# A reordering of a mixture-of-experts stage's blocks, with the next stage's first preparing moved beside its last nine, and four instead of six load seats

## What is computed

```python
x = x + 0.5 * ffn(layernorm(x))     # mixture of experts
x = x + attention(layernorm(x))     # 16 heads of 8, q = k = v
x = x + 0.5 * ffn(layernorm(x))     # the same mixture again

def ffn(x):                         # 4096 tokens, 8 experts, each token goes to its best 2
    xf = layernorm(x, ln_g, ln_b)
    scores, idx = top_k(xf @ router_w, 2)
    gate = softmax(scores)
    # expert e on its tokens: z = layernorm(xf, eg, eb)
    # x2 = clip(z @ W2 + b2); hidden = clip((z @ W1 + b1) * silu(x2)); y = clip(hidden @ Wo + bo)
    return sum over the two experts of gate * y
def attention(x):
    q = (x @ W_qkv.T) split in 16 heads
    return softmax(q q^T / sqrt(8)) q, heads joined, @ W_o.T
```

## Time and profile before

| | us |
|---|---|
| median of 3 runs | 1426.98 |
| the profiled execution's own time | 1427.73 |
| its span, first to last instruction | 1426.0 |
| first block's rows transposed | 108.3 |
| last transposing back of the first mixture | 330.47 |
| first row maximum of the attention on VectorE | 371.76 |

### The profile page before, as it was taken

How to read it: one execution, slowest core, us unless ns; L and a number is a source line. 1 busy time by engine, 2 the same in 40 slices (tenths; PEclk the granted TensorE clock), 3 DMA queues, 4 the chain that set the end, 5 groups by cost and what they waited for, 6 DMA issues and landing times.

```text
span 1426.0 us, 29423 instructions
## 1 busy us (share of the span) xinstructions
PE 1248.9 (88%) x10053; PEld 649.7 (46%) x10053; DVE 1170.2 (82%) x2305; ACT 896.2 (63%) x1876; POOL 511.2 (36%) x595
## 2 busy tenths in 40 slices
PE   3738999984389999999999999999999988889992
PEld 3727888872022222322323323233322247778882
DVE  8876788876698899889898988988899458868885
ACT  1214555552058888888778887788877865545651
POOL 3875333334433000243335324351434023433331
PEclk9999999996589999999999999999999999999997
DMA  8126545451311201102111011011101312445555
GB/s 260 38 71 217 203 180 191 178 204 34 104 51 35 72 19 35 36 24 66 36 40 48 17 57 36 17 52 36 36 3 32 113 62 101 161 170 186 188 204 192
DMA packets 65382, 135.58 MB, mean 95 GB/s; under 512 B 13330, under 2 KB 34932, under 8 KB 65204
## 3 DMA queue, kind: packets, MB, share of 16 engines
q1 hardware_dynamic: 56196, 116.18, 23.7%
q0 software_dynamic: 8704, 16.93, 3.7%
q10 hardware_dynamic: 336, 0.59, 0.1%
HBM read 47.35 MB, written 25.07 MB: 51 GB/s over the span
## 4 chain that ended last, share of the span: by engine, by line
PE 44%; DVE 21%; DMA 3%; issue 3%; ACT 3%; SPq 1%; POOL 0%; ACTq 0%; POOLq 0%; DVEq 0%
PE psum L2067 13%; DVE att_neg_part L1753 11%; PE psum L2043 7%; PE psum L2047 5%; PE psum L2024 5%; PE psum L1971 3%; PE psum L1959 3%; PE psum L1961 3%; DVE att_neg_part L1758 2%; DVE stats L1426 1%; ACT att_probs L1326 1%; DMA y_dram<-ffn_y,ffn_block_rows 1%; PE psum L2090 1%; ACT att_o_t L1341 1%; DMA ffn_rec<-record 1%
## 5 line engine op out<-in xcount | busy, mean ns | idle before, releaser
L1326 ACT ACTIVATE att_probs<-psum 128x512 f32<-128x512 f32 x1024 | 556.5, 596 | 119.3 <-PE psum L2049 90.3
L1753 DVE TENSOR_REDUCE att_neg_part<-psum 128x2 f32<-128x1024 f32 x441 | 532.0, 1223 | 69.0 <-PE psum L2025 56.0
L2067 PE MATMUL psum<-att_probs,att_values 128*16 128x256 f32 x4096 | 321.4, 386 | 6.3 <-ACT att_o_t L1341 4.2
L1281 ACT ACTIVATE ffn_silu<-ffn_x2c,ffn_rec 128x256 f32<-128x256 f32 (+1 forms) x320 | 154.6, 487 | 163.3 <-DVE ffn_x2c L1689 162.6
L1143 POOL DMA_INDIRECT y_dram<-ffn_y,ffn_block_rows x144 | 142.1, 987 | 274.5 <-ACT ffn_y L1299 248.7
L2024 PE MATMUL psum<-att_right,att_left 64*128 64x512 bf16 x512 | 198.3, 388 | 27.5 <-DMA att_right<-q_parts_dram 15.9
L2043 PE MATMUL psum<-att_right,att_left 64*128 64x512 bf16 x512 | 198.6, 388 | 4.9 <-DVE att_neg_part L1753 4.8
L2046 PE MATMUL psum<-att_right,att_left 64*128 64x512 bf16 x512 | 198.5, 388 | 4.0 <-DVE att_neg_part L1753 2.1
L1689 DVE TENSOR_SCALAR ffn_x2c<-psum,ffn_rec 128x256 f32<-128x256 f32 (+1 forms) x320 | 162.8, 513 | 45.9 <-PE psum L1961 41.7
L2025 PE MATMUL psum<-att_right,att_left 64*128 64x512 bf16 x512 | 198.9, 389 | 0.0
L2047 PE MATMUL psum<-att_right,att_left 64*128 64x512 bf16 x512 | 193.7, 378 | 0.0
(11 more groups left out here) (198 smaller groups left out, 1514.4 us busy)
## 6 DMA issues: line engine op xcount, KB each, us to landing
ffn_rec<-record SPq DMA_DIRECT2D x80, 776.5 KB, 3.7
ffn_block_rows<-rows_dram SPq DMA_DIRECT2D x64, 130.0 KB, 2.2
att_left<-q_parts_dram SPq DMA_DIRECT2D x64, 96.0 KB
att_right<-q_parts_dram SPq DMA_DIRECT2D x120, 48.0 KB
record<-in_L_ffn_W SPq DMA_DIRECT2D x16, 256.0 KB, 6.5
last_y<-y_dram SPq DMA_DIRECT2D x8, 512.0 KB, 7.4
att_right<-q_parts_dram SPq DMA_DIRECT2D x90, 32.0 KB
y_dram<-ffn_y,ffn_block_rows POOLq DMA_INDIRECT x144, 2.6
```

The source lines that it names most:

```text
L1326: S.activation(probs[:, slot % PROBS, :], ring_bank(("score", slot))[:, :], ACT.Exp, scale=SCALE).then_inc(att_bank.by_act, 1)
L1753: last = V.tensor_reduce(out=neg_part[:, h % 2, keys, p::PAIR, t], in_=psum[:, low:high + 1, :], axis=AX.X, op=ALU.max, negate=True)
L2067: last = TE.matmul(value_bank[head * VS:head * VS + VW, q], values[:, b % 2, kt, team * TEAM + head, :], probs[:, (UNIT * n + j) % PROBS, ...
```

## The change

1. **Order of blocks.** The 8 singles now stand at i = 23 to 30 (`SINGLES`), and 9 pairs follow. Among an expert's pairs, those that hold rows of the first batch come first, so that everything of the first batch is done when block 30 is. The layout on VectorE works with 16 instead of 8 running sums for this. Both mixtures use this order.
2. **Seats.** The first mixture has 4 seats instead of 6 (`SLOTS = (4, 6)`), its buffers lie elsewhere in SBUF so that the attention's first operands fit beside them; the second keeps 6.
3. **Loads.** `sync_next_block` now loads the weights as soon as the seat's old block is `biased`, and then waits for its scatter to load the rows. Before, both waited for the scatter, and the rows came first.
4. **Chores.** The first batch's preparing (`PREPARED`) becomes a list `HEAD`: GpSimd's first blankings stand beside blocks 23 to 26, steps 0 to 15 beside blocks 34 to 38. SyncE loads the first batch's results behind the load of block 34, and the first team's operands behind the load of block 39. The two attention weights are loaded and transposed at the program's start.

```diff
-    SECTIONS = [slice(0, EARLY), slice(EARLY, PAIRS), slice(PAIRS, BLOCKS)]
-    SLOTS = 6
+    LEFT = E - 2
+    SINGLES = slice(EARLY + LEFT, EARLY + LEFT + E)
+    SECTIONS = [slice(0, EARLY), slice(EARLY, SINGLES.start), SINGLES, slice(SINGLES.stop, BLOCKS)]
+
+    KINDS = [(BH, 0, 0), (BH, 1, 0), (1, 2, 0), (BH, 1, LEFT)]
+    SLOTS = (4, 6)
...
-        def seat(i):
+        def seat(k, i):
-            return (i - 1) % SLOTS
+            return (i - 1) % SLOTS[k]
...
+        HEAD = [[] for _ in range(HC * (BLOCKS - SINGLES.start))]
+        for n in range(4):
+            HEAD[4 * n].append(("blank", n, 0, WHOLE))
+        at = HC * E
+        for step, half, slot in ((0, 0, 15), (1, 0, 15), (0, 1, 16), (1, 1, 16), (2, 0, 17), (2, 1, 18), (11, 0, 23), (11, 1, 25)):
+            HEAD[at + slot].append(("prepare", 0, step, (half, 2)))
+        for step, slot in ((3, 19), (5, 20), (7, 21), (9, 22), (13, 27), (15, 28)):
+            HEAD[at + slot].append(("prepare", 0, step, WHOLE))
...
             for i in range(EARLY, BLOCKS):
                 sync_next_block(k, i)
+                if k == 0 and i == SINGLES.stop + SLOTS[0] - 1:
+                    sync_first_results()
+            if k == 0:
+                sync_first_team()
...
         def sync_next_block(k, i):
-            n = k * BLOCKS + i - SLOTS
-
+            n = k * BLOCKS + i - SLOTS[k]
+
+            Q.wait_ge(biased, n + 1)
+            sync_load_record(k, i)
             Q.wait_ge(scattered_y[n % YSETS], y_scatters(n + 1, n % YSETS))
             sync_load_rows(k, i)
-            sync_load_record(k, i)
...
-            pool_blank_values(0)
-            pool_blank_left(0)
-            for chore in PREPARED:
-                pool_chore(*chore)
-            pool_blank_right(0)
-            G.wait_ge(split_done, 1)
-            pool_blank_values(1)
             for s in range(1, OPERANDS):
                 pool_blank_left(s)
                 pool_blank_right(s)
```

More of the change, by code:

```diff
@@ L244, in build_macaron @@
         first = ExitStack()
-        sets.extend(RouteSet(k, first) for k in range(1, B - 1))
-        beyond = sbuf("beyond_the_blocks", [P, 4096], owner=first)
-        sets.append(RouteSet(B - 1, first))
+        last_set = RouteSet(B - 1, first)
         VEC = 2 * E + 2 * E * HC + E
@@ L337, in build_macaron @@
         laid_out = semaphore("laid_out")
-        block_in = [semaphore(f"block_in{s}") for s in range(SLOTS)]
         scattered_y = [semaphore(f"y_scattered{r}") for r in range(YSETS)]
@@ L782, in sync_experts @@
                 sync_load_rows(0, 0)
-                for i in range(1, SLOTS):
+                for i in range(1, SLOTS[0]):
                     if i >= 2:
@@ L789, in sync_experts @@
                 sync_fillers(0)
-            for i in range(SLOTS, EARLY):
+            for i in range(SLOTS[k], EARLY):
                 sync_next_block(k, i)
@@ L1006, in pool_program @@
             for n in range(2):
-                for some, tiles in zip(SECTIONS, (BH, BH, 1)):
-                    G.iota(blocks_i[:, n, some], pattern=[[tiles if n else 1, some.stop - some.start]], base=0,
-                           channel_multiplier=0)
+                for some, (tiles, _, past) in zip(SECTIONS, KINDS):
+                    G.iota(blocks_i[:, n, some], pattern=[[tiles if n else 1, some.stop - some.start]],
+                           base=past * (tiles if n else 1), channel_multiplier=0)
             G.iota(spares_i[:, :], pattern=[[1, BH]], base=RESULTS, channel_multiplier=BH)
@@ L1073, in pool_chore @@
                 G.tensor_tensor(rows, rows, projected(half), ALU.add).then_inc(x_by_pool, 1)
+            elif what == "blank" and which < 2:
+                pool_blank_values(which)
+            elif what == "blank" and which == 2:
+                for lane in sets[B - 1].rows_out:
+                    G.wait_ge(lane, 16 * BT)
+                pool_blank_left(0)
+            elif what == "blank":
+                pool_blank_right(0)
             elif what == "mix":
@@ L1356, in scalar_chore @@
                 h = (step // 2 - 1) % 2
-                S.wait_ge(*att_bank.full(("prepare", which, step)))
+                S.wait_ge(*when_full(("prepare", which, step)))
                 if which > 1:
@@ L1970, in tensor_second @@
             for c in range(HC):
-                last = TE.matmul(y_bank[n % 2][:, few], rec[:, s, WO + c * F:WO + (c + 1) * F], hidden[:, n % 2, c, few],
+                last = TE.matmul(y_bank[n % 2][:, few], mix[k].rec[:, s, WO + c * F:WO + (c + 1) * F], mix[k].hidden[:, n % 2, c, few],
                                  start=(c == 0), stop=(c == HC - 1))
```

302 lines of the change are left out of this document (167 added, 135 removed).

## The result

The changed kernel takes 1521.59 us, median of 4 runs (1518.04 to 1527.56), against 1426.82 for the kernel before, also 4 runs. The ratio is 1.0666, 95% interval 1.0628 to 1.0704. The profiled execution took 1527.56 us, its span is 1525.8 (1426.0 before).

What follows compares the result with a forecast made beforehand. TensorE bounds the first mixture at 5.62 us a pair; four seats would bind instead at 9.0. Terms 3.8 + 108.5 + 7.5 + 8 - 36.7 + 7.8 + 2 = +100.9 gave 1528 us, range 1490 to 1565.

Steps and rivals of the forecast that it cites:

- The seat's cycle: First mixture: weighing, scatter, row load, transposing and copy close over one block with four seats; 9.0 us per pair against 5.62.
- Singles: First mixture's single blocks: steps of 7.1 us among themselves, 8.6 or 7.5 where singles and pairs meet.
- Chores: Preparing moved beside the first mixture's last blocks: the first rstd holds block 32's scatter some 5.6 us; +8, ends 3 and 16.
- Middle: First mixture, block 4's to block 39's transposing: +116.5 us, from +108.5 for the steps and +8 for chores.
- The hole: Between the first mixture's last landing and the first row maximum: closed whole, operands loaded ahead; -36.7 us.
- Drain: Block 39's transposing to the last landing: 21.8 us with a pair, against 14.3 with a single; +7.5.
- The attention's start: First row maximum to first score: 34.9 instead of 27.1 us, SyncE's loads standing behind GpSimd's blanking; +7.8.
- GpSimd's blankings: Beside the first mixture's blocks: two of 1.8 us each time fit between scatters, whose two issues take 2.3 of 9.0 us.
- Second mixture: Six seats kept: drain grows by 7.5 us, earlier weights are credited 5.5; +2, ends -5 and +8.
- The pace holds: Rival, first mixture: landing and loading stay hidden, steps stay at 5.62 us or the singles' pace; 1418 us, chance 7%.
- The clock falls as well: Rival, first mixture: waits drop TensorE to half clock, steps of 11.2 us; +53, 1581 us, chance 5% for the large loss.
- A lighter load makes landings shorter: Rule against the trace, scatter landings: slower pace shortens them to 2.1 us, giving 1511 instead of 1528 us.

Runs made afterwards that it cites:

- the seats mended: Changed kernel with separate row seats in the first mixture, weights kept at four: five row seats 1.0026, six with weights issued early 1.0013 of the kernel before.

## Why the prediction was right, point by point

- **The seat's cycle, 9.0 us per pair.** Right in mechanism, 5% long. Measured 8.53: weighing to request 5.66 (taken 5.96), request to transposing 2.13 (2.2), to the copy 0.47 (0.48), to the weighing 0.27 (0.37). That the circle closes over one block is shown by the runs: 8.7 us with four seats in either order, 5.62 with five or six. The 0.3 in the first part lie behind the second scatter's issue: from there to the rows' request it is 2.97 instead of 3.27. The landing goes with it: over 140 to 300 us the view of the line has 2.2/2.3/3.4 (least, median, most), in the kernel before over the same stretch 2.2/2.7/5.6.
- **Start, +3.8.** +2.0: from the first transposing to block 4's it is 3.6 us more, but the first transposing itself came 1.65 earlier.
- **Singles.** Steps of 8.05 behind pairs and 6.5 to 6.8 among themselves, forecast 8.6 and 7.1: the same 0.5. The step to block 26 is the exception (9.66).
- **Chores, +8 (3 to 16).** Mis-sized, inside its ends. The blocks 35 and 36 took 10.8 and 19.2, some 13 us more than plain steps. The place was right (block 32's scatter behind the first rstd); that scatter was 9.3 us late instead of 5.6. Block 35's rows, too, were requested 8.0 us behind the weighing of block 31, right behind the loads of the first batch's results in SyncE's list; that these held them up was not tested by itself.
- **Middle, +116.5 in all.** +114.6, and that close a hit is in part luck. At the 0.5 us that the circle was forecast too long, 35 steps would have been 17 us shorter; they were 7 shorter, because steps here and there took longer than the circle (9.3 to 10.3 us to blocks 5, 9, 22, 26 and 39), for which the forecast had no term. The chores' 5 us too little made up for most of the 7.
- **The hole, -36.7.** -36.8: the operands were there.
- **Drain, +7.5.** +8.2 in the first mixture; in the second, last transposing to the end is 41.4 us instead of 32.9, +8.5.
- **The attention's start, +7.8.** +9.0, and its cause, SyncE behind the third blanking, shown by moving one line: -6.6.
- **GpSimd's blankings "fit between the scatters".** This step was wrong: they hold VectorE. It cost little here only since the pace was not VectorE's; at TensorE's pace it is 7 us.
- **Second mixture, +2.** +0.2, but not as summed. From its first to its last transposing it takes 218.6 us instead of 226.9, which gives the longer drain back. Some 6 of these 8.3 us lie behind block 22, where the order differs, so they come with the order that makes the drain longer. Only 2.3 lie in the steps before, where the earlier weights can be seen: the steps to blocks 14 and 15 are 4.5 us shorter, the step to block 9 is 2.5 longer. The credit of 5.5 for the weights is not shown. Not forecast were the 2.7 us in the rest of the attention; their cause stays open.
- **The pace holds.** Its premise is out. Its price of 1418 was too low besides: with the seats mended the ratio is 1.001 to 1.003, 1429 to 1431 us, not 0.993, since chores and blankings cost more than the 10 us taken at full pace.
- **The clock falls as well.** It fell, to 0.90 over the middle and 0.65 and 0.78 in short stretches behind waits of 2.7 us, but the cold work fitted into the circle's slack, as the forecast said that part of a step would. It cost 0.1 to 0.2 us a step.
- **TensorE's busy share of about 0.6.** It was 0.75 (37.64 of 50 us), since the sign was reckoned at full clock: 5.62 of 8.68 us is 0.65, and the slow matmuls fill more of the step.
- **A lighter load makes landings shorter.** By what the Trainium skill (DMA: Bandwidth & Descriptors, section "Latency and other measured facts") says, landings should get shorter at the slower pace. The trace agrees in sign: 2.3 us against 2.7 in the median over 140 to 300 us, with 128 GB/s instead of 184 over 200 to 250. The least landing, 2.2, is the same in both, and the time came out between the 1511 of that rule and 1528.

## What to carry to other kernels

Count seats by the whole circle, from the load to the event that frees the seat and back to the load, and divide by the number of blocks over which an engine's own order closes it; then give seats only to what is in the circle (rows, 1.0 KB) and not to what is large (weights, 6.2 KB). Work moved out of a hole is not free beside full engines: here 36 us were closed and 34 came back beside the last blocks, and the gain came only when the moved work also had its place in each queue that it shares (GpSimd's scatters, SyncE's loads). In an in-order list, put what is ready early ahead of what waits.

## What the runs showed that was not expected

A GpSimd memset holds VectorE's clips from SBUF to SBUF until it ends: 2.50 us instead of 0.29 beside a memset of 1.84, 2.31 instead of 0.43 beside another. It is not so every time: in the same profile a clip at 277.37 took 0.70 instead of 0.43 and ended long before the memset recorded at 277.86. The two long clips are recorded 0.50 and 0.19 us ahead of their memsets, so which of the two engines was first is not settled by these records. Cutting the memsets in four shortened the waits to a piece. The Trainium skill (SBUF — State Buffer, section "Who interferes with whom") has this rule: the two engines share a pair of ports under a lock that is held for a whole instruction, and `tensor_scalar` can enter the mode that takes it. The two long clips agree with it, with the numbers above, and so does the clip that only reads PSUM, which was not held; the clip at 277.37 leaves the order of the two engines open.

The second: one wait of 1.0 to 2.7 us in each step of 8.5 us already lowers the granted clock in part (0.90 over 50 us), and 1.88 us of idle matmuls in it bring it back to 1.00, yet the time hardly moves when a circle of transfers sets the pace.
